# Finer waits in a linear-attention chunk loop, and a softmax bound computed in blocks of 2048

## What is computed

```python
xn = layernorm(x)
# linear attention, 8 heads of 128
q, k, v = xn @ Wq.T, xn @ Wk.T, xn @ Wv.T
o = causal_linear_attention(q, k, v)      # state += k^T v, chunk by chunk
denom = max(abs(sum(q * cumsum(k))), 1)
s = rmsnorm_per_head(o / denom) @ Wo.T
# feed-forward branch
h = xn + mla(rmsnorm(xn))                 # softmax attention, 16 heads of 64, causal
h = h + moe(rmsnorm(h))                   # 8 experts, top 2, 1024 -> 2048 -> 1024
y = x + s * silu(h)
```

## Time and profile before

| | |
|---|---|
| three timed runs | 4942.89, 4944.91, 5031.77 us; median 4944.91 |
| profiled execution | 4941.29 us, span of its slowest core (core 0) 4939.8 us |
| spans of the eight cores | 4916.5 to 4939.8 us |
| mean granted clock of TensorE | 0.760 to 0.762 on all cores |
| busy, core 0 | PE 3167.9 us (64%), DVE 1084.4 us (22%), ACT 1069.3 us (22%) |

### The profile page before, as it was taken

One profiled execution on the slowest core, in us unless ns is written; L12 is line 12 of the kernel. 1 busy time (PEld: TensorE's weight loads), 2 busy tenths in 40 slices (PEclk: granted clock), 3 DMA queues, 4 the chain that ended last, 5 costly groups with the idle time before them and its releaser, 6 DMA issues.

```text
span 4939.8 us, 42736 instructions; the slowest of 8 cores (4916.5 to 4939.8 us)
## 1 busy us (share of the span) xinstructions
PE 3167.9 (64%) x13297; PEld 1262.6 (26%) x13297; DVE 1084.4 (22%) x2066; ACT 1069.3 (22%) x1463; POOL 43.6 (1%) x65
## 2 busy tenths in 40 slices
PE   0373333333742665666655429999999999999960
PEld 0132111112310111111111214444444444444430
DVE  4201333330032333333332221001110001110012
ACT  3231011011312333333332111111111111111111
POOL 0000000000000000000000000000000000000000
PEclk9985566665965555555555759999999999999985
DMA  4312000003100000000001140303040303123014
GB/s 146 89 18 39 13 9 13 13 13 56 22 5 0 0 0 1 1 0 1 0 1 33 44 77 1 52 17 69 1 69 1 69 1 68 32 37 53 17 45 159
DMA packets 56029, 158.58 MB, mean 32 GB/s; under 512 B 4224, under 2 KB 5248, under 8 KB 55808
## 3 DMA queue, kind: packets, MB, share of 16 engines
q0 software_dynamic: 39248, 95.54, 11.0%
q1 hardware_dynamic: 16560, 60.30, 3.6%
HBM read 209.42 MB, written 33.55 MB: 49 GB/s over the span
## 4 chain that ended last, share of the span: by engine, by line
PE 59%; DVE 17%; DMA 8%; issue 8%; ACT 5%; DVEq 1%; ACTq 1%; SPq 0%; POOLq 0%; PEldq 0%
PE pA L157 28%; PE pB L157 22%; PE pw L157 6%; DVE p2lb L895 4%; DMA p4s<-s_sp 2%; PE pt L162 2%; DMA p0x<-x 1%; ACT p2pb L843 1%; PE ps L157 1%; DVE p1o1f L549 1%; DVE p2pb L855 1%; DVE p2tmp L788 1%; DVE p2omla L901 1%; DMA s_sp<-p1sout 1%; ACT p2sq L782 1%
## 5 line engine op out<-in xcount | busy, mean ns | idle before, releaser
L157 PE MATMUL pB<-p3w,p3hid 128*128 128x512 bf16 x4096 | 889.2, 379 | 37.5 <-ACTq L96 35.1
L157 PE MATMUL pA<-h3T,p3w 128*128 128x512 bf16 x4096 | 891.7, 380 | 0.0
L1074 ACT ACTIVATE p3hid<-pA 128x512 bf16<-128x512 f32 x512 | 305.7, 597 | 1474.5 <-PE pA L157 1474.5
L157 PE MATMUL pw<-p2pb,p2vaug 128*65 128x512 bf16 x640 | 335.0, 626 | 356.7 <-DVEq L96 356.7
L1096 DVE SCALAR_TENSOR_TENSOR acc<-pB,p3comb,acc 128x512 f32<-128x512 f32 x256 | 192.2, 751 | 1618.0 <-PE pB L157 1615.3
L157 PEld LDWEIGHTS pB<-p3w,p3hid 128*128 128x128 bf16 x4096 | 398.5, 98 | 528.2 <-issue 52.4
L157 PEld LDWEIGHTS pA<-h3T,p3w 128*128 128x128 bf16 x4096 | 401.3, 98 | 484.8 <-issue 3.3
L895 DVE RECIPROCAL p2lb<-ps 64x512 f32<-64x512 f32 x64 | 214.4, 3350 | 209.4 <-PE ps L157 209.4
L843 ACT ACTIVATE p2pb<-pA,p2nmub 128x1024 bf16<-128x1024 f32 x160 | 178.1, 1113 | 335.9 <-PE pA L157 335.9
L157 PEld LDWEIGHTS pw<-p2pb,p2vaug 128*65 128x65 bf16 x640 | 60.1, 144 | 629.6 <-issue 629.6
L162 PE MATMUL pt<-ident,p1o2b 128*128 128x128 bf16 x128 | 16.2, 306 | 290.6 <-DVEq L96 290.6
(11 more groups left out here) (156 smaller groups left out, 1856.4 us busy)
## 6 DMA issues: line engine op xcount, KB each, us to landing
p3w<-w POOLq DMA_DIRECT2D x16, 4096.0 KB, 27.1
p0x<-x SPq DMA_DIRECT2D x16, 512.0 KB, 4.2
xn_sp<-p0xn SPq DMA_DIRECT2D x16, 512.0 KB, 3.0
h_sp<-p0h1b POOLq DMA_DIRECT2D x16, 512.0 KB, 2.9
s_sp<-p1sout SPq DMA_DIRECT2D x16, 512.0 KB, 2.6
p2xnr<-xn_sp SPq DMA_DIRECT2D x16, 512.0 KB, 3.3
p4x<-x SPq DMA_DIRECT2D x16, 512.0 KB, 4.8
p4s<-s_sp SPq DMA_DIRECT2D x16, 512.0 KB, 5.6
```

Source lines behind the costliest of these rows:

```text
L157: t.matmul(o, l, r, start=st, stop=sp), sig=sig)
L1074: e.activation(hv[:, m, :], pb[:, 0:512], AF.Silu), sig=True)
```

## The change

There are two parts.

In the chunk loop the waits at the end of an iteration (line 612) are taken out. In their place TensorE waits, before each write or read in the next iteration, for the mark of the instruction that last used the buffer: line 549 before the V projection, the copy into p1oTc before the K transposes, the copies into p1sout before the scores, the copy out of pw and the state update before the output and the state matmuls. VectorE waits for the transposes of the chunk before ahead of o2b, ScalarE for the output projection of the chunk before ahead of p1oTc, and VectorE for the landing of the previous write to s_sp ahead of the copies into p1sout. A certify follows these copies.

In the bound loop p2sq grows from 512 to 2048 columns. A pass now handles all 2048 tokens of a block: four squares, four matmuls into pA and pB in place of pw, two maxima over 1024 elements each and two running maxima. There are 16 passes, each waiting for the one before.

```diff
 
     for t_ in (state_f, state_b, carry_f, carry_b):
         sch.emit("vector", lambda e, t=t_: e.memset(t[:, :], 0.0), sig=(t_ is carry_b))
+    sch.certify("vector")
     sch.wait("tensor", sch.mark("vector"))
+    m_o1read = m_qzread = m_ots_p = m_state_p = m_sout_p = m_ot_p = m_sp_p = m_ssp_p = None
 
     for ci in range(NTI):
         par = ci % 2
         t0, t1 = ci * 128, (ci + 1) * 128
 
+        if m_o1read is not None:
+            sch.wait("tensor", m_o1read)
         for sl in range(2):
             for k in range(DK):
                 mmi(c, c.ps[sl][:, 0:512], xv[:, k, t0:t1], wvv[:, k, sl * 512:(sl + 1) * 512],
@@ -462,6 +466,8 @@
         sch.certify("scalar")
         m_vs = sch.mark("scalar")
 
+        if m_ots_p is not None:
+            sch.wait("tensor", m_ots_p)
         for h in range(AH):
             tri(c, c.pt[:, 128 * h:128 * (h + 1)], kTv[:, h, t0:t1], sig=(h == AH - 1))
         sch.wait("scalar", sch.mark("tensor"))
...
+        if m_sout_p is not None:
+            sch.wait("tensor", m_sout_p)
         for h in range(AH):
             pb = c.ps[2 + h // 4]
             mmi(c, pb[:, 128 * (h % 4):128 * (h % 4 + 1)], kTv[:, h, t0:t1], qTv[:, h, t0:t1],
@@ -500,6 +508,10 @@
         sch.wait("tensor", m_scm)
         sch.wait("tensor", m_vs)
         sch.wait("tensor", m_ks)
+        if m_qzread is not None:
+            sch.wait("tensor", m_qzread)
+        if m_state_p is not None:
+            sch.wait("tensor", m_state_p)
         for h in range(AH):
             ob = c.ps[h // 4][:, 128 * (h % 4):128 * (h % 4 + 1)]
             qb = c.pw[:, h:h + 1]
@@ -536,9 +550,11 @@
             sch.emit("vector", lambda e: e.tensor_copy(carry_b[:, :], carry_f[:, :]), sig=True)
             sch.certify("vector")
         m_state = sch.mark("vector")
+        m_state_p = m_state
 
         sch.wait("vector", m_o)
         sch.emits("vector", lambda e: e.tensor_copy(qzf[:, :], c.pw[:, 0:AH]))
+        m_qzread = sch.mark("vector")
...
@@ -549,6 +565,7 @@
                      e.tensor_scalar_mul(o1f[:, 128 * h:128 * (h + 1)],
                                          pb[:, 128 * (h % 4):128 * (h % 4 + 1)],
                                          rdn[:, h:h + 1]), sig=(h == AH - 1))
+        m_o1read = sch.mark("vector")
         sch.wait("scalar", sch.mark("vector"))
...
             sch.emit("vector", lambda e, h=h:
                      e.tensor_scalar_mul(o1f[:, 128 * h:128 * (h + 1)],
                                          o1f[:, 128 * h:128 * (h + 1)], rst8[:, h:h + 1]))
+        if m_ot_p is not None:
+            sch.wait("vector", m_ot_p)
         sch.emit("vector", lambda e: e.tensor_tensor(o2b[:, :], o1f[:, :], c.normw[:, :],
                                                      OP.mult), sig=True)
         sch.certify("vector")
@@ -584,32 +603,41 @@
         for k in range(DK):
             tri(c, c.pt[:, 128 * k:128 * (k + 1)], o2b[:, 128 * k:128 * (k + 1)],
                 sig=(k == DK - 1))
+        m_ot_p = sch.mark("tensor")
+        if m_sp_p is not None:
+            sch.wait("scalar", m_sp_p)
         sch.wait("scalar", sch.mark("tensor"))
         sch.emit("scalar", lambda e: e.copy(oTc[:, :], c.pt[:, :]), sig=True)
         sch.certify("scalar")
-        sch.wait("tensor", sch.mark("scalar"))
+        m_ots_p = sch.mark("scalar")
+        sch.wait("tensor", m_ots_p)
         for sl in range(2):
             pb = c.ps[2 + sl]
             for k in range(DK):
                 mmi(c, pb[:, 0:512], oTc[:, 128 * k:128 * (k + 1)],
                     wov[:, k, sl * 512:(sl + 1) * 512], k == 0, k == DK - 1,
                     sig=(k == DK - 1))
-        sch.wait("vector", sch.mark("tensor"))
+        m_sp_p = sch.mark("tensor")
+        sch.wait("vector", m_sp_p)
+        if m_ssp_p is not None:
+            sch.wait("vector", m_ssp_p)
         for sl in range(2):
             sch.emit("vector", lambda e, sl=sl:
                      e.tensor_copy(sout[:, sl * 512:(sl + 1) * 512], c.ps[2 + sl][:, 0:512]),
                      sig=(sl == 1))
+        sch.certify("vector")
         m_sout = sch.mark("vector")
+        m_sout_p = m_sout
         sch.wait("sync", m_sout)
         m_ssp = sch.dmas("ssp", lambda s, ci=ci:
                          s.dma_start(c.D["s_sp"].ap()[ci * 128:(ci + 1) * 128, :], sout[:, :]))
+        m_ssp_p = m_ssp
...
-        sch.wait_all("tensor", m_state, m_sout, sch.mark("scalar"), m_ssp)
 
     sch.barrier()
     pes.close()
@@ -762,35 +790,49 @@
     sch.certify("vector")
     sch.wait("tensor", sch.mark("vector"))
 
-    sq2 = sb("p2sq2", [128, 512], BF16, stack=pesQ)
+    sq2 = sb("p2sq2", [128, 2048], BF16, stack=pesQ)
     qkmax = sb("p2qkmax", [1, 2 * DK], F32, stack=pesQ)
     tmp1 = sb("p2tmp1", [1, 1], F32, stack=pesQ)
     mubb = sb("p2mubb", [1, DK], BF16, stack=pesQ)
     nmub = sb("p2nmub", [128, DK], F32, stack=pesQ)
     sch.emit("vector", lambda e: e.memset(qkmax[:, :], 0.0), sig=True)
+    sch.certify("vector")
     sch.wait("scalar", sch.mark("vector"))
     if not c.p2_mub:
         sch.emits("vector", lambda e: e.memset(nmub[:, :], 0.0))
         sch.certify("vector")
         sch.wait("tensor", sch.mark("vector"))
         sch.wait("scalar", sch.mark("vector"))
+    mubmark = None
     for which, src in (((0, qv), (1, kv)) if c.p2_mub else ()):
         for m0 in range(DK):
+            sch.wait("scalar", sch.mark("vector"))
             for sl in range(4):
-                sch.wait("scalar", sch.mark("vector") if (m0 + sl) else sch.mark("vector"))
-                sch.emit("scalar", lambda e, s=src[:, m0, sl * 512:(sl + 1) * 512]:
-                         e.activation(sq2[:, :], s, AF.Square), sig=True)
-                sch.certify("scalar")
-                sch.wait("tensor", sch.mark("scalar"))
-                mmi(c, c.pw[0:1, 0:512], c.onesb[:, 0:1], sq2[:, :], True, True, sig=True)
-                sch.wait("vector", sch.mark("tensor"))
-                col = which * DK + m0
-                sch.emits("vector", lambda e: e.reduce_max(tmp1[:, :], c.pw[0:1, 0:512],
-                                                           axis=AX.X))
-                sch.emit("vector", lambda e, col=col:
-                         e.tensor_max(qkmax[:, col:col + 1], qkmax[:, col:col + 1],
-                                      tmp1[:, :]), sig=True)
-                sch.wait("vector", sch.mark("vector"))
+                sch.emit("scalar", lambda e, s=src[:, m0, sl * 512:(sl + 1) * 512], sl=sl:
+                         e.activation(sq2[:, sl * 512:(sl + 1) * 512], s, AF.Square),
+                         sig=True)
+            sch.certify("scalar")
+            if mubmark is not None:
+                sch.wait("tensor", mubmark)
+            sch.wait("tensor", sch.mark("scalar"))
+            for sl in range(4):
+                PS = c.pA if sl < 2 else c.pB
+                mmi(c, PS[0:1, (sl % 2) * 512:(sl % 2) * 512 + 512], c.onesb[:, 0:1],
+                    sq2[:, sl * 512:(sl + 1) * 512], True, True, sig=(sl == 3))
+            sch.wait("vector", sch.mark("tensor"))
+            col = which * DK + m0
+            sch.emits("vector", lambda e: e.reduce_max(tmp1[:, :], c.pA[0:1, 0:1024],
+                                                       axis=AX.X))
+            sch.emits("vector", lambda e, col=col:
+                      e.tensor_max(qkmax[:, col:col + 1], qkmax[:, col:col + 1],
+                                   tmp1[:, :]))
+            sch.emits("vector", lambda e: e.reduce_max(tmp1[:, :], c.pB[0:1, 0:1024],
+                                                       axis=AX.X))
+            sch.emit("vector", lambda e, col=col:
+                     e.tensor_max(qkmax[:, col:col + 1], qkmax[:, col:col + 1],
+                                  tmp1[:, :]), sig=True)
+            sch.certify("vector")
+            mubmark = sch.mark("vector")
     if c.p2_mub:
         sch.emits("vector", lambda e: e.tensor_mul(qkmax[:, 0:DK], qkmax[:, 0:DK],
                                                    qkmax[:, DK:2 * DK]))
```

## The result

The changed kernel's median over ten executions is 4802.15 us, eight of them took 4798.6 to 4806.5 us, and the predicted time was 4800 us in a range of 4776 to 4836. Against the kernel before the ratio is 0.9714, 95% interval 0.9701 to 0.9727: 2.9% faster, about 141 us.

A forecast was written before the change was run, and what follows sets the result against it. Chains of engines taking turns bound the two changed loops. The chunk loop's 70.2 us wait and 32.2 us clock and the bound loop's 40.9 us take 143.3 us off 4941.3; with 2 added, 4800 us, range 4776 to 4836.

The forecast's parts named there:

- The total and the two shares: Chunk loop 102.4 us and bound loop 40.9 us less, 143.3 us in all; 4800 us forecast.
- The wait: Chunk boundary: idle time behind the s_sp transfer goes, 4.68 us at 15 boundaries, 70.2 us.
- the cover: Chunk boundary: copies into p1sout finish during the next V projection, at least 1.4 us before the scores need them.
- The rival that used it up: Chunk loop: scores wait for the p1sout copies; at four times their length 3.1 us a boundary lost, 4846 us; chance 0.02.
- The V projection's clock: Chunk loop: V projection at clock 1.00 instead of 0.50, 3.48 us instead of 5.63, 32.2 us less at 15 boundaries.
- The rest of the chunk: Chunk loop: output projection unchanged near 94 us, about 8 us more gain as upper bound; other new waits cost nothing.
- everything else: Larger p2sq, certifies after the memsets and the copies: under 1 us in all.
- has no reason to leave: Chunk loop: without the idle stretch TensorE enters the V projection at 1.00 and stays there; 2.15 us less each boundary.
- The bound loop: Bound loop: 16 passes of 8.76 us, 140.2 us, 40.9 us less; bounds of the saving 20 to 55 us.
- The rivals: Five other outcomes: V projection's clock not granted 0.12, bound-loop hand-overs 0.05, current limit 0.04, replacing wait 0.02, slower expert stage 0.03.
- The 13/16 clock: Chunk loop: current limit under dense work on all cores lowers the V projection's clock to 13/16; 4812 us; chance 0.04.
- the trace disagrees: Expert stage: clock 1.00 with eight cores at work, against the 13/16 limit, which would make the sum 12 us smaller.

The follow-up runs named there:

- the pair of runs with the clock held: Extra matmuls in all idle stretches of the chunk loop: changed kernel with bound loop in halves, 4669.6 us; kernel before with its wait kept, 4859.2 us.
- the kernel with the densest TensorE work: Changed kernel with the bound loop in halves and extra matmuls in the chunk loop's idle stretches: 4669.6 us at best, ratio 0.9406.

## Where the prediction was right and where it was wrong

**The total and the two shares: right.** Predicted 102.4 us from the chunk loop and 40.9 from the bound loop; measured 102.1 and 42.2 in the profiles, and 101.3 and 41.6 with each part alone.

**The wait: right at the boundary.** 4.68 us at 15 boundaries was the sum; the pair of runs with the clock held gives 4.69 there and 4.47 net. No new wait took its place: the scores are not idle, and the cover, given as at least 1.4 us without the transposes, is 1.6 to 1.8 with them. The rival that used it up was priced at 4846 us for copies of four times their length; with such copies the kernel took 4860 us. The V projections were to be 37.6 us apart and are 37.54: that of chunk 1 starts at 477.50 and that of chunk 15 at 1003.11 us, (1003.11 - 477.50) / 14.

```profile
477.50 3.62 PE L157 MATMUL pA<-p1wvT,xnT 128*128 128x512 bf16 x16
...
1003.11 3.62 PE L157 MATMUL pA<-p1wvT,xnT 128*128 128x512 bf16 x16
```

**The V projection's clock: right.** 1.00 throughout, 3.45 us from its start to the transposes (3.48 predicted), 60.8 us of busy time (58 predicted; each shows 3.62 us with its overlap, and the first, behind an idle stretch, 6.5), and filling the gap of the kernel before gave the same length without touching the wait.

**The rest of the chunk: wrong, and this is the step that failed.** The prediction priced the clock in one stage, the V projection, and put the rest of the chunk at no change: the output projection was to stay near 94 us, with at most 8 us of gain as a bound, the output matmuls weren't named, and the new waits ahead of them were worth "nothing". All three moved. By the distances between starts, means of the 14 periods on core 0, the period lost 6.88 us: 4.69 are the idle stretch of the boundary and 5.57 - 3.45 = 2.12 the V projection, as predicted; 5.69 - 4.88 = 0.81 are the output projection (82.0 us of busy time, 11.9 less, outside the bound). Against that, output matmuls at the slow clock take 0.54 us more, and they start 0.18 us later behind the masking (2.7 us in all, where the prediction had under 1 us for everything else). This last distance is 3.84 to 3.86 us in every kernel with the new waits and 3.65 or 3.66 in every one with the old; no run takes the waits out one by one. So 0.81 us gained and some 0.7 lost were both missing from the sum, and that they nearly cancel is luck. The treatment of the clock as a price of one stage was the error: a gain or a loss of it in one stage moved it in others. Speeding the output matmuls slowed the output projection, an idle stretch of 2.2 us cost the clock in every other chunk, and 2.96 us of waiting ahead of the scores lengthened the period by 3.38. A sentence of the prediction, that TensorE "has no reason to leave" the fast clock, was true up to the scores only; the 3.9 us of masking behind them are such a reason.

**The bound loop: right, term by term.** Two passes' starts in the changed kernel are 8.68 us apart (8.76 predicted):

```profile
1308.00 2.79 ACT L812 ACTIVATE p2sq<-p2qT 128x512 bf16<-128x512 bf16 x4 [5.89 <-DVEq L96]
...
1311.08 1.01 PE L157 MATMUL pA<-p2sq,onesb 128*1 128x512 bf16 x2 [6.81 <-ACTq L96]
...
1311.88 1.06 PE L157 MATMUL pB<-p2sq,onesb 128*1 128x512 bf16 x2
...
1313.12 1.21 DVE L824 TENSOR_REDUCE p2tmp<-pA 1x1 f32<-1x1024 f32 x1 [5.45 <-PE pB L157]
1314.50 0.15 DVE L827 TENSOR_TENSOR p2qkmax<-p2qkmax,p2tmp 1x1 f32<-1x1 f32 x1 [0.17 <-DVE p2tmp L824]
1314.82 1.21 DVE L829 TENSOR_REDUCE p2tmp<-pB 1x1 f32<-1x1024 f32 x1 [0.17 <-DVE p2qkmax L827]
1316.20 0.15 DVE L832 TENSOR_TENSOR p2qkmax<-p2qkmax,p2tmp 1x1 f32<-1x1 f32 x1 [0.17 <-DVE p2tmp L829]
1316.68 1.35 ACT L812 ACTIVATE p2sq<-p2qT 128x512 bf16<-128x512 bf16 x2 [5.89 <-DVEq L96]
```

Four squares 2.79 us (2.79), 0.29 to the first matmul (0.29), 2.04 from there to the first maximum (1.31 + 0.76 = 2.07), 1.21 for a maximum (1.21), 0.33 back to ScalarE (0.38).

**The rivals.** None occurred in the changed kernel's profiled execution. The 13/16 clock of the Trainium skill ("TensorE: Matmul & The Clock Gate", Part 1) did not show in the profiled execution of the kernel with the densest TensorE work either: 1.00 in a window of 556 us on core 0, and mean clocks of 0.815 to 0.818 on all eight cores, above those of any other kernel here. But it did show in the expert stage of another run, on one die only. These are the same 85 us of the kernel before with the gap filled, first on core 5, then on core 0:

```profile
3705.00:3790.00 85.00, 83.77 (x320) 34.56 (x319) 8.60 (x12) 9.55 (x16) 0.00 (x0) 0.81 0.00 1
```

```profile
3705.00:3790.00 85.00, 82.72 (x384) 37.20 (x383) 11.25 (x15) 10.33 (x18) 0.00 (x0) 1.00 0.00 1
```

So the prediction's "the trace disagrees" holds for the core and the execution that it read, and no further; all eight cores were in this stage in both cases, and what decides was not tried.

## What to carry to other kernels

An idle stretch on TensorE has two prices, its length and the clock that it costs the work behind it, and the second can be half of the first: here 67 us of length with the clock held, and 32 by the sum or 26 by the run that filled the gap, for a wait shown as 67.8 us. The two come to 93 of the 102 us, since filling the gap shortened the output projection by 0.2 us a chunk and taking the wait out by 0.8. The second price can't be summed stage by stage, for what one stage gains another can lose; read the granted clock over a whole period, and test by filling idle stretches with extra matmuls. In a loop where the engines take turns, batching saves the hand-overs (42 us here), and letting each engine wait only for the half that it overwrites saves the turns (another 79 us).

## What the runs showed of the hardware

Two things were not expected. The same idle stretch of 2.16 us before the V projection was followed by a projection at full clock in one chunk and by one that took 5.3 us in the next, in strict alternation over the loop. And the mean periods of the chunk loop did not move with the idle time that was put in or taken out: 37.44 and 37.54 us with and without 1.25 us of gain in the output and state matmuls, 40.96 and 40.92 with 2.3 and 3.1 us more of waiting. With the clock held it is 34.46. These are no fixed set either: it is 36.22 us with both idle stretches filled, where chunks of 34.3 and of 37.4 us mix, and 42.65 with the gap of the kernel before filled, where 41.9 and 43.3 alternate. Why just these periods is left open.
